# The second sweep's loop with eight steps in its body, and eight behind it, in place of four

## What is computed

```python
# layer 0: degree-normalised graph convolution
h = x @ weight
out = segment_sum((deg_inv_sqrt[src] * deg_inv_sqrt[dst])[:, None] * h[src], dst) + bias
x = layernorm(x + out)
# layer 1: attention over edges, 8 heads of 16
w = mlp(edge_attr_64, rad_*) + mlp(edge_attr_32, sph_*)      # hidden width 256, silu
q, k, v = (x @ wq)[dst], (x @ wk)[src], (x @ wv)[src]
alpha = (q * w * k).sum(axis=-1) / sqrt(16) * edge_weight[:, None]
x = layernorm(x + segment_sum(alpha[..., None] * v, dst) / 16)
```

## Time and profile before

| | us |
|---|---|
| median of three runs | 1775.34 (1770.6 to 1778.68) |
| profiled execution, its own time | 1772.56 |
| its span, first to last instruction | 1770.7 |
| first to last start of a gather of the second sweep | 667.4 to 1735.7 |
| the loop of the second sweep on TensorE, end of its first turn to its exit | 826.9 to 1673.5 |

### The profile page before, as it was taken

One profiled execution on the slowest core, in us unless ns is written; L12 is line 12 of the kernel. 1 busy time (PEld: TensorE's weight loads), 2 busy tenths in 40 slices (PEclk: granted clock), 3 DMA queues, 4 the chain that ended last, 5 costly groups with the idle time before them and its releaser, 6 DMA issues.

```text
span 1770.7 us, 45707 instructions
## 1 busy us (share of the span) xinstructions
PE 1571.4 (89%) x12986; PEld 1454.2 (82%) x12986; DVE 1379.2 (78%) x3869; ACT 924.5 (52%) x1399; POOL 1298.8 (73%) x1249
## 2 busy tenths in 40 slices
PE   3389999899899978999999999999999999999995
PEld 2278888888888866889988898989898898888984
DVE  8986777777777566887887788887888777888886
ACT  1144555554555374555555555555555555555563
POOL 8777777777777627777777777777777777777771
PEclk9999999999999988999999999999999999999997
DMA  3133333333333266666666666666666666666663
GB/s 100 43 104 101 107 105 99 106 105 99 106 105 100 77 166 160 178 177 175 181 178 172 175 174 176 179 176 184 178 176 179 177 175 172 172 178 176 180 181 105
DMA packets 177657, 259.26 MB, mean 146 GB/s; under 512 B 80694, under 2 KB 91757, under 8 KB 177436
## 3 DMA queue, kind: packets, MB, share of 16 engines
q0 software_dynamic: 51840, 132.72, 27.8%
q1 hardware_dynamic: 120008, 120.99, 24.4%
q10 hardware_dynamic: 5716, 4.55, 0.9%
HBM read 235.32 MB, written 22.79 MB: 146 GB/s over the span
## 4 chain that ended last, share of the span: by engine, by line
POOL 43%; issue 18%; DVE 14%; PE 14%; DVEq 4%; DMA 3%; POOLq 1%; SPq 1%; ACT 1%; ACTq 1%
POOL arena L657 40%; PE bank L948 5%; PE bank L991 4%; DVE count L1342 4%; POOL rel L620 3%; DVE xsplit L1309 2%; DVE key_hot L1330 2%; PE bank L958 2%; DVE low_hot L1329 2%; DVEq L1315 1%; DMA arena<-kv_d,idx 1%; DMA xraw<-in_sph_t 1%; DVEq L1342 1%; PE bank L930 1%; POOLq L674 1%
## 5 line engine op out<-in xcount | busy, mean ns | idle before, releaser
L657 POOL DMA_INDIRECT arena<-kv_d,idx x808 | 823.3, 1019 | 264.4 <-issue 262.3
L948 PEld LDWEIGHTS bank<-w,hid 128*128 128x128 f32 x6464 | 779.9, 193 | 24.0 <-ACT hid L773 1.5
L948 PE MATMUL bank<-w,hid 128*128 128x128 f32 x6464 | 788.7, 277 | 0.0
L773 ACT ACTIVATE hid<-bank,b 128x512 f32<-128x512 f32 x808 | 495.6, 683 | 308.3 <-PE bank L932 301.7
L657 POOL DMA_INDIRECT arena<-xs_d,idx x408 | 394.5, 967 | 139.8 <-issue 121.0
L930 PE MATMUL bank<-xsplit,w_hi 128*128 128x512 f32 x808 | 344.8, 437 | 79.1 <-ACT hid L773 54.5
L765 ACT ACTIVATE xsplit<-xraw 64x1024 fp32r<-64x1024 f32 x202 | 212.4, 1052 | 239.0 <-DMA xraw<-in_sph_t 224.1
L1309 DVE TENSOR_TENSOR xsplit<-xraw,xsplit 64x256 fp32r<-64x256 f32 x808 | 287.9, 413 | 6.6 <-ACT xsplit L765 0.2
L930 PEld LDWEIGHTS bank<-xsplit,w_hi 128*128 128x128 f32 x808 | 154.7, 191 | 113.2 <-ACT hid L773 63.4
L1342 DVE TENSOR_TENSOR count<-count,bank 128x200 f32 x400 | 144.5, 361 | 124.8 <-issue 57.9
L958 PE MATMUL bank<-onehot,late 128*128 128x126 f32 x1616 | 215.0, 281 | 6.3 <-DVE late L1519 4.5
(11 more groups left out here) (144 smaller groups left out, 1310.6 us busy)
## 6 DMA issues: line engine op xcount, KB each, us to landing
late<-relrow_d SPq DMA_DIRECT2D x103, 256.0 KB
xraw<-in_rad_t SPq DMA_DIRECT2D x205, 128.0 KB
xraw<-in_sph_t SPq DMA_DIRECT2D x410, 64.0 KB
w_sb<-w_d SPq DMA_DIRECT2D x52, 256.0 KB, 4.0
w_d<-w_sb SPq DMA_DIRECT2D x51, 256.0 KB
arena<-kv_d,idx POOLq DMA_INDIRECT x808
arena<-xs_d,idx POOLq DMA_INDIRECT x408
qwin<-q_d SPq DMA_DIRECT2D x101, 31.5 KB
```

The lines of the kernel that those rows point to most:

```text
L657: pool.indirect_dma_start(gath[:, k, t * width:(t + 1) * width], None, table, bass.IndirectOffsetOnAxis(ap=idx[:, pair.slot(4), j * TILES ...
L773: act.activation(hid[:, s.slot(2), c, :], hid_ps[s.sub(4, c, 4 * s.total).slot(len(hid_ps))][:, :], ACT.Silu, bias=b0[:, c:c + 1]).then_in ...
L948: mm = pe.matmul(w_ps[:, t * D:(t + 1) * D], hid[:, b, c, t * P:(t + 1) * P], w1[:, c, :], start=False, stop=(c == 3), skip_group_check=True)
```

## The change

The two constants that cut the second sweep's loop are raised. The same 51 steps run in the same order on every engine, with the same buffers and the same waits. Three stand ahead of the loop, 40 are in five turns of eight, and eight stand behind it.

```diff
 UNROLL = 4
 FIRST, LAST = 3, 2
 UNROLL1, LAST1 = 8, 8
-UNROLL2, LAST2 = 4, 4
+UNROLL2, LAST2 = 8, 8
 CHUNK = 4
```

## The result

The changed kernel takes 1780.96 us in the median of 13 runs (1773.5 to 1784.6), the kernel before 1773.12 (median of 13). One of those 13 runs of the kernel before took 2772.29 us and is left out of the ratio; the other twelve lie between 1768.95 and 1779.8, with a median of 1772.56. The ratio, of the means, is 1.0037 with a 95% interval of 1.0023 to 1.0052: slower by some 6.6 us. That is inside the 0.5% that the prediction counted as no change, and clear of zero all the same. The profiled execution took 1783.31 us with a span of 1781.5, 10.8 us over that of the earlier trace rows.

The account below looks back on a forecast made before the run. GpSimd's row of gathers was taken as the bound: 667.4 + 1069.2 + 34.1 = 1770.7 us of span, with 0 added by the change, so 1772.6 against its own execution and 1775.3 against the median; predicted 1775, range 1768 to 1784.

Parts of the forecast that it names:

- What bounds the kernel: Whole run: GpSimd's 808 gathers with their pauses, 1069.2 us, between a start of 667.4 and a tail of 34.1.
- Fewer branches: Second sweep: six fewer back branches save 3 us on VectorE and 2.2 us on TensorE, 0 on the path.
- A longer body: Second sweep's loop: code reloads at four branches delay VectorE and TensorE 3.3 to 5.0 us each, covered by GpSimd's gathers.
- the rule about taken branches: Loop's back branches: a taken branch to code outside what is held stalls until fetched; 3.3 us per reload on VectorE.
- second rival: Second sweep's back branches: reload stalls come onto the path, +10 us, or +30 with TensorE's upper bound; chance 0.08.
- half-clock stretch: TensorE behind a reload gap: clock at 0.50 for 3.4 us, adding 1.7 us to the delay.
- TensorE's wait for hid: Second sweep: TensorE's total wait for ScalarE's hid, 44.9 us before, shrinks by about what the stalls cost.
- GpSimd feels it only through s_msg: Second sweep: stalls reach GpSimd only by message buffers; least room 16.6 us, so delays up to 11.6 don't reach it.
- third rival: GpSimd's gathers: some 64 us of stretching shifts by one seventh, 9 us either way; chance 0.03 faster, 0.04 slower.
- The prediction's own sign of being wrong: GpSimd: waits for line 1519 growing beyond 0.3 us each, or a gather's mean moving by over 10 ns.
- VectorE's work is the same: Second sweep, within the gathers' length rival: VectorE's work beside the gathers is unchanged but shifted by its stalls.
- The first rival: Second sweep: reloads come onto the path if TensorE and VectorE also set the pace, +10 us, 1785.5; chance 0.08.

Follow-up runs that it names:

- e2: Kernel before with two steps in the second sweep's body and four behind it, 22 turns: ratio 0.9994 to the kernel before.
- e12: Kernel before with eight steps in the body and eight behind it on TensorE and VectorE only, other engines four: ratio 1.0034 to the kernel before.
- e5: Kernel before with eight steps on TensorE and VectorE only, run where the kernel before took 2492.3 us: ratio 1.0075 to it.
- e9: Kernel before with VectorE's two-input message replaced by a one-input sum of about the same length, results incomplete: ratio 0.9843 to the kernel before.
- e3: Kernel before with eight steps in the body and eight behind it on TensorE's loop only, others four: ratio 1.0031 to the kernel before.
- e4: Kernel before with eight steps in the body and eight behind it on VectorE's loop only, others four: ratio 1.0023 to the kernel before.
- e11: Kernel before, four steps in the body, with 14 extra TensorE matmuls at the start of each of eleven turns: ratio 1.0053 to the kernel before.

## Why the prediction was right or wrong

**What bounds the kernel** held. The sum of 808 gathers, their pauses and two fixed ends gives the changed kernel too, to 0.3 us.

**Fewer branches: 0 on the path** held (e2).

**A longer body** held in kind. (The prediction calls the rule about taken branches its second rival; it is the first in its list.) VectorE's reload was taken at 3.3 us and was 3.7. TensorE's, for which there was no row, was taken at 3.3 and was 4.0, with the half-clock stretch behind it as said. ScalarE, which I left out because 144 operations a turn are fewer than VectorE's 161, reloads too: four idle times of 2.2 us. Operations alone were the wrong count: with waits, register work and branches the trace has 331 records in ScalarE's turn of eight steps, and 312 in VectorE's turn of four, which stayed in place. e12 has the change's cost without ScalarE's reload. GpSimd didn't reload. TensorE's wait for hid fell from 44.9 to 31.9 us, as forecast.

**"GpSimd feels it only through s_msg" is the step that failed.** It was right that no wait would appear: the room, from the end of a message to the first gather that needs its buffer, fell from 16.6 to 14.9 us at its least, far from zero. But the argument took the length of a gather as given and asked only whether GpSimd would be kept waiting. GpSimd also feels VectorE while both work, and where in a gather a message falls is moved by the very delays that I had called covered. The price came out as the third rival, "the gathers' own length moves", to which I gave 0.04 on the slow side, with 79 ns of stretching in the earlier trace rows in hand and no look at what caused it. The prediction's own sign of being wrong, a mean that moves by over 10 ns, came true: 1019 to 1032 ns over the whole span. Sorting the gathers of before by their place to a message would have shown the lever. The half of my argument that "VectorE's work is the same" was no protection: the same messages stretched 21 more gathers.

**The size.** I predicted 1775 and no change; measured were 1781 and a factor of 1.0037 with 1 outside the interval. That 1781 lies within the range of 1768 to 1784 is no merit of the mechanism. The range's lower end is the profiled execution, 1772.6, less 4.5; from 1770.6, as it is told, it would be 1766. The first rival had its stalls in the right place and a price of 10 us, but its mechanism, a starved GpSimd, didn't take place here. GpSimd was starved in e5.

**Open** is why a shift by 3 to 4 us makes things worse and not just different. In e9, 14 gathers start within 0.1 us of the replaced message's start, about what chance gives (202 x 0.1 / 1.29 = 16). Before there are 42 and after 63, but only 22 in e2. A part of the pull can be read in the rows at 1004 us above. A gather stretched to 1.45 us and the pause of 0.30 put the next gather 1.75 us later, and the next message starts 1.74 us after the last, so that the second gather is caught as the first was. Of the 42, 12 are followed by another of the kind in the gather right behind, of the 63 it is 22, of e2's 22 it is 4 and of e9's 14 none. That the delays of e3, e4, e11 and e12 add to it on average is what the ratios say; none of the runs shows how.

## What to carry to other kernels

An engine that never waits can still be slowed by its neighbours: look at the spread of its instructions, not only at its idle time, and find out what the long ones overlap before calling a stall elsewhere covered. Where a loop body is small enough to stay in place, a longer one buys nothing from branches that were hidden and here added a reload behind each taken branch; 22 turns of two steps ran as well as 11 of four. Here the lever was the message: with a one-input instruction in its place the kernel was 1.6% faster, if a form of it could be found that still computes it.

## What was not expected of the hardware

A reload behind a taken branch idles VectorE for 3.7 us, TensorE for 4.0 us and ScalarE for 2.2 us, at bodies of eight steps, and VectorE idles at most 0.5 us behind the branch of the body of four that stays in place. A gather of 942 ns takes up to 1.48 us when a VectorE product of two SBUF tensors runs at its start, and 948 ns beside a reduction of one tensor of the same length. Beside a product of the same length and output whose second input lies in PSUM it is 949 ns at most (957 in the changed kernel). And 22 to 76 gathers of 808 start within 0.1 us of the message in the kernels that have it and aren't held up by the readers, where chance gives 16.
